# Contextual attention: straight-line loops, exponentials written twice, and a shifted addition done by an accumulating DMA

## The reference

```python
raw_w, Hr, Wr = _extract_patches(b, kernel, RATE * STRIDE)   # 4x4 patches, step 2
f = b[:, :, ::RATE, ::RATE]                                  # 40x40
w, Hs, Ws = _extract_patches(f, KSIZE, STRIDE)               # 3x3 patches of f
norm = jnp.sqrt(jnp.sum(w * w, axis=(2, 3, 4), keepdims=True))
wn = (w / jnp.maximum(norm, ESCAPE)).reshape(B, L, C * KSIZE * KSIZE)
yi = jnp.einsum('bpd,bld->blp', xf, wn) * mm
yi = jax.nn.softmax(yi * SOFTMAX_SCALE, axis=1) * mm
patches = jnp.einsum('blp,bld->bpd', yi, raw_w.reshape(B, L, C * kernel * kernel))
# overlapping 4x4 patches are added up at step 2, and the sum is divided by 4
```

## Time and profile before

| | us |
|---|---|
| median of 3 runs | 1543.32 (1543.14 to 1550.75) |
| the profiled execution | 1549.3 |
| its span, first to last instruction | 1547.5 |
| TensorE busy | 1389.9 |
| VectorE busy | 1226.9 |
| ScalarE busy | 860.8 |
| GpSimd busy | 54.6 |

### The profile page before, as it was taken

How to read it: one execution, slowest core, us unless ns; L and a number is a source line. 1 busy time by engine, 2 the same in 40 slices (tenths; PEclk the granted TensorE clock), 3 DMA queues, 4 the chain that set the end, 5 groups by cost and what they waited for, 6 DMA issues and landing times.

```text
span 1547.5 us, 28187 instructions
## 1 busy us (share of the span) xinstructions
PE 1389.9 (90%) x7190; PEld 906.0 (59%) x7190; DVE 1226.9 (79%) x2831; ACT 860.8 (56%) x2233; POOL 54.6 (4%) x63
## 2 busy tenths in 40 slices
PE   4978999889998899988999889997999889999896
PEld 4755655656557565565656566565665656556333
DVE  4668888778888788887898777977779788887983
ACT  2676555646557465583555644656545655557431
POOL 1001000010000100001000000001000010000100
PEclk9998999999999999999999999998999999999998
DMA  5305352273522653145631545315462153522442
GB/s 97 44 1 152 96 119 73 61 161 86 114 66 78 153 105 104 50 108 134 122 87 45 130 113 116 86 51 138 106 120 76 50 148 92 120 66 81 124 137 60
DMA packets 181676, 149.67 MB, mean 97 GB/s; under 512 B 119986, under 2 KB 177394, under 8 KB 181490
## 3 DMA queue, kind: packets, MB, share of 16 engines
q1 hardware_dynamic: 181170, 146.60, 39.8%
q10 hardware_dynamic: 320, 0.99, 0.3%
HBM read 19.76 MB, written 13.11 MB: 21 GB/s over the span
## 4 chain that ended last, share of the span: by engine, by line
PE 40%; DVE 18%; issue 13%; SPq 12%; ACT 8%; DMA 6%; DVEq 1%; ACTq 1%; POOL 0%; POOLq 0%
PE psO L511 18%; PE psG L461 17%; SPq L307 5%; DVE G L921 4%; DVE G L861 4%; DVE S L867 3%; DMA SH<-G 3%; PE psG L470 3%; DVE Z L954 3%; ACT S L680 3%; DVE G L932 3%; SPq L255 3%; SPq L295 2%; DMA HV<-LOHI 2%; ACT G L666 2%
## 5 line engine op out<-in xcount | busy, mean ns | idle before, releaser
L511 PE MATMUL psO<-Z,B 123*128 123x492 f32 (+1 forms) x1792 | 768.0, 557 | 41.8 <-ACT OSB L700 22.6
L511 PEld LDWEIGHTS psO<-Z,B 123*128 123x128 f32 x1792 | 327.5, 195 | 266.7 <-issue 179.5
L461 PE MATMUL psG<-LH,HL 128*123 128x246 f16 (+2 forms) x2616 | 411.0, 287 | 26.2 <-issue 19.7
L461 PEld LDWEIGHTS psG<-LH,HL 128*123 128x123 f16 x2616 | 280.5, 138 | 166.2 <-issue 112.5
L867 DVE CUSTOM_DVE_ANT_0 S<-G,RB 123x492 f32<-123x492 f32 (+1 forms) x448 | 268.9, 606 | 94.4 <-DVE G L861 53.9
L691 ACT ACTIVATE G<-G,nb 123x492 f32<-123x492 f32 (+1 forms) x448 | 270.2, 649 | 106.7 <-DVE G L921 105.9
L680 ACT ACTIVATE S<-S,nm 123x480 f32<-123x480 f32 (+3 forms) x560 | 306.7, 553 | 4.2 <-DVE nm L872 4.1
L921 DVE SCALAR_TENSOR_TENSOR G<-G,RA,psB 123x492 f32<-123x492 f32 (+1 forms) x448 | 275.2, 657 | 20.5 <-issue 19.6
L932 DVE TENSOR_TENSOR G<-G,SH 123x492 f32<-123x492 f32 (+1 forms) x448 | 251.4, 600 | 42.9 <-DMA SH<-G 42.5
L666 ACT ACTIVATE G<-psG 123x492 f32<-123x492 f32 (+3 forms) x256 | 120.3, 473 | 216.1 <-PE psG L461 127.4
L653 ACT ACTIVATE G<-psG 123x246 f32<-123x246 f32 (+1 forms) x136 | 64.4, 474 | 262.5 <-PE psG L461 262.2
(11 more groups left out here) (84 smaller groups left out, 585.7 us busy)
## 6 DMA issues: line engine op xcount, KB each, us to landing
SH<-G SPq DMA_DIRECT2D x336, 214.8 KB
SH<-G SPq DMA_DIRECT2D x112, 107.2 KB
SH<-G SPq DMA_DIRECT2D x336, 19.2 KB
XP<-x SPq DMA_DIRECT2D x20, 280.0 KB, 6.0
XP<-mid SPq DMA_DIRECT2D x20, 280.0 KB, 5.3
mid<-OSB SPq DMA_DIRECT2D x52, 80.0 KB, 2.3
out<-OSB SPq DMA_DIRECT2D x52, 80.0 KB, 2.3
HL<-LOHI SPq DMA_DIRECT2D x16, 246.5 KB, 3.5
```

Of the source, the lines that this page charges most:

```text
L461: last = pe.matmul(psG[0:TW, bank, b0 * TW:b1 * TW], st[:, p:p + TW], mv[:, lo:lo + n], start=i == 0, stop=i == len(terms) - 1)
L511: last = pe.matmul(psO[:, b, 0:n], B[:, o:o + 128], Z[:, 2 * (s % 2) + j, 0:n], start=t == 0, stop=t == TILES - 1)
```

## The change

There are two parts. All loops over units are written out: `Fori` becomes `for` on all engines. And the shifted addition is done in another way. ScalarE now makes each exponential twice: first into a buffer `Y` (four of them, where `SH` was), then in place in `G`. GpSimd issues a DMA that *adds* `Y`, moved by one partition and one column, to `G` (`accum_op=ALU.add`), one DMA of 122 rows per tile. `shift_pair` on SyncE and `add_shifted` on VectorE are gone. Who waited for `y1_made` (VectorE's count) now waits for the landing of the DMAs, `y1_in`, by the tile's buffer. ScalarE waits, before it writes a `Y` buffer, for the landing of the DMA four tiles earlier.

```diff
             def softmax_pair(at):   # ScalarE
                 for j, t in enumerate(arg_tiles(i)):
-                    act.wait_ge(arg_made, u * NB + k * TILES + 2 * i + j + 1)
-                    act.sem_inc(act_gate, 1)
+                    o = k * TILES + 2 * i + j
+                    if u * NB + o >= SFREE:
+
+                        act.wait_ge(*y1_done(u, o - SFREE))
+                        act.sem_inc(act_gate, 1)
+                    act.wait_ge(arg_made, u * NB + o + 1)
+                    act.activation(Y[:, o % SFREE, 0:n], G[:, t * GLEN + c0:t * GLEN + c0 + n], ACT.Exp,
+                                   bias=nb[:, bass.ds(u * TILES + t, 1)]).then_inc(y_copied, 1)
+                for j, t in enumerate(arg_tiles(i)):
+                    act.wait_ge(y_copied, u * NB + k * TILES + 2 * i + j + 1)
                     y = G[:, t * GLEN + c0:t * GLEN + c0 + n]
                     act.activation(y, y, ACT.Exp, bias=nb[:, bass.ds(u * TILES + t, 1)]).then_inc(y_made, 1)
...
-            with act.Fori(0, UNITS - 2) as u:
+            for u in range(UNITS - 2):
                 body(u, u + 1, u + 2)
...
-            def add_shifted(at):   # VectorE
-                for j, t in enumerate(arg_tiles(i)):
-                    o = k * TILES + 2 * i + j
-                    dve.wait_ge(sh_in[o % SFREE], (u * (NB // SFREE) + o // SFREE + 1) * 16 * len(SHIFT_PARTS))
-                    g = G[:, t * GLEN + c0:t * GLEN + c0 + n]
-                    dve.tensor_tensor(g, g, SH[:, o % SFREE, 0:n], ALU.add).then_inc(y1_made, 1)
...
             def sum_pair(at, s):
-                dve.wait_ge(y1_made, u * NB + k * TILES + min(2 * i + 3, TILES) + SFREE)
-                dve.sem_inc(dve_gate, 1)
+
+                for o in range(2 * i + 1, min(2 * i + 3, TILES)):
+                    dve.wait_ge(*y1_done(u, k * TILES + o))
+                    dve.sem_inc(dve_gate, 1)
...
-                pool.wait_ge(y1_made, u * NB + 2 * i + 2 + SFREE)   # GpSimd, wrap
-                pool.sem_inc(pool_gate, 1)
+                for o in (2 * i, 2 * i + 1):
+                    pool.wait_ge(*y1_done(u, o))
+                    pool.sem_inc(pool_gate, 1)
...
+            def add_shifted(at):   # GpSimd
+                u, k, i = at
+                c0, n = p_cols(k)
+                for j, t in enumerate(arg_tiles(i)):
+                    o = k * TILES + 2 * i + j
+                    g = t * GLEN + c0
+                    pool.wait_ge(y_made, u * NB + o + 1)
+                    pool.dma_start(G[1:TW, g + 1:g + n], Y[0:TW - 1, o % SFREE, 0:n - 1],
+                                   accum_op=ALU.add).then_inc(y1_in[o % SFREE], 16)
+
             def body(u, v):
                 for s in BODY:
+                    at = place(u, v, s + LEAD)
+                    if at:
+                        add_shifted(at)
                     if s < 5 and u is not None:
                         wrap(u, s + 2)
```

More of the change, by code:

```diff
@@ L106, in contextual_attention @@
         RB = sb("RB", [TW, TILES * TW], F32)
-        SH = sb("SH", [TW, SFREE, 4 * TW], F32)
+        Y = sb("Y", [TW, SFREE, 4 * TW], F32)
         SHJ = sb("SHJ", [TW, 4 * TW], F32)
@@ L190, in contextual_attention @@
         arg_made = sem("arg_made")
+        y_copied = sem("y_copied")
         y_made = sem("y_made")
-        sh_in = [sem(f"sh_in{i}") for i in range(SFREE)]
+        y1_in = [sem(f"y1_in{i}") for i in range(SFREE)]
         shj_in = sem("shj_in")
-        y1_made = sem("y1_made")
         z_made = sem("z_made")
@@ L202, in contextual_attention @@
         SQ_STEPS = 4
-        CLEARED = 10
+        CLEARED = 9
         MROWS = HALF + 1
@@ L219, in arg_tiles, with y1_done @@
             return [(2 * i + TILES - 1) % TILES, 2 * i]
+        def y1_done(u, o):
+            return y1_in[o % SFREE], (u * (NB // SFREE) + o // SFREE + 1) * 16
         def place(u, v, s):
@@ L312, in shift_strip @@
                 c0, n = p_cols(k, True)
-                sp.wait_ge(y1_made, u * NB + k * TILES + 1 + SFREE)
+                sp.wait_ge(*y1_done(u, k * TILES))
                 sp.sem_inc(sp_gate, 1)
@@ L329, in body @@
                         lay_out_features(w, ("HL", "LH", "H1", "HV"))
-                    at = place(u, v, s + LEAD)
-                    if at:
-                        shift_pair(at)
                     at = place(u, v, s + 2)
@@ L341, in body, with source @@
                             store_chunk(u, NK - 1, dst)
[L343 to L346, removed]
+            def source(u):
+                return None if u is None else (x, mid)[u // IMAGES][u % IMAGES]
             sp.sem_inc(stored, 16)
@@ L360, in _ @@
             xp_read(0)
[L361 to L369, removed]
+            body(None, 0, 1, source(1), source(0), None)
+            for u in range(UNITS):
+                v, w = (n if n < UNITS else None for n in (u + 1, u + 2))
+                body(u, v, w, source(w), source(v), (mid, out)[u // IMAGES][u % IMAGES])
             sp.wait_ge(stored, (UNITS * sum(N_OUT) + 1) * 16)
@@ L573, in _ @@
             body(None, 0, 1)
-            with pe.Fori(0, UNITS - 2) as u:
+            for u in range(UNITS - 2):
                 body(u, u + 1, u + 2)
@@ L963, in body @@
                         argument_pair(at)
-                    at_y = place(u, v, s + AHEAD)
-                    if at_y:
-                        add_shifted(at_y)
                     at_z = place(u, v, s + 1)
@@ L1037, in _ @@
             body(None, 0, 1)
-            with dve.Fori(0, UNITS - 2) as u:
+            for u in range(UNITS - 2):
                 body(u, u + 1, u + 2)
@@ L1070, in _ @@
             body(None, 0)
-            with pool.Fori(0, UNITS - 1) as u:
+            for u in range(UNITS - 1):
                 body(u, u + 1)
```

17 lines of the change are left out of this document (1 added, 16 removed).

## The result

The changed kernel takes 1602.4 us in the median (1596.0 to 1606.1) where the kernel before takes 1543.9 on the same chip: 1.0364 times as long [1.0315, 1.0414]. The forecast was 1517, faster, so its direction was wrong. The profiled execution has a span of 1604.3 us against 1547.5, 56.8 more.

The account below looks back on a forecast made before the run. TensorE was taken as the limit for most of each unit, ScalarE in short pieces, TensorE's jump between looped units. 1549.3 - 19.5 (loops) + 3 (units) - 10 (last unit) = 1522.8, less 6.0 for the median: 1517 us, range 1497 to 1700.

Parts of the forecast that it names:

- Ends: 17 us, if the layout DMAs land about half a microsecond later beside heavier transfers: Handover between units: low end of the gain from written-out loops; 19.5 us was taken, 22 the other end.
- 12.6 us of engine time for 234 KB: DMA engine time of one addition at 18.5 GB/s per engine: 0.8 us over sixteen engines, 6.3 over two.
- are not queued behind those issues, though they share the engines: Once per unit, new DMAs avoid the wait on SyncE behind the next image's rows: -1 us, seven times -7.
- I take 2.1 to 3 us: Last unit: flight of an adding DMA, within a round of about 6 to 7 us for two pairs.
- +3 us: Inside the units: chunk 3 pieces +10, squares pair +2.4, two score pairs -2.6, shifted copies -7; ends -10 and +20.
- The squares pair: Pair with the next image's squares: ScalarE adds 1.3 us where 0.9 is free, +0.4, six times +2.4.
- The pair with two score pairs: Mid-unit pair: VectorE falls to 5.2 us, ScalarE rises to 6.7 and takes its place; -0.4, seven times -2.6.
- I take 19.5: Handover between units: gain in us from removing TensorE's five jumps back, with ends of 17 and 22.
- -7: Once per unit, shifted copies stand on SyncE behind the next image's rows, costing TensorE about 1 us; seven times -1.
- the second: Rival, chance 0.14: GpSimd's issue is dear, setting the last unit's pace from 1.66 us; 1569 us at 2.68.
- the third: Rival, chance 0.11: jumps return as fetch stalls, or ScalarE's cost mid-unit equals the loops' gain; 1536 to 1544 us.
- The first (two engines per addition): Rival, chance 0.20: each addition's DMA gets two engines, lengthening flight to 7.6 or 13.9 us; mostly 1566 to 1850 us.

Follow-up runs that it names:

- With copies: The changed kernel with plain copies of the same bytes in place of all adding DMAs (addition left out): 1527.8 us, 0.9880 of the kernel before.
- the loops alone: The kernel before with `Fori` written out as a Python `for` on all five engines, nothing else changed: 1505.5 us, 0.9746 of the kernel before.
- exponentials of one column: The changed kernel with ScalarE's exponential into Y covering one column in place of up to 492, adding DMAs whole: 1584.9 us, 1.0262 of the kernel before.

## Why the prediction was wrong

**The failing step: "Ends: 17 us, if the layout DMAs land about half a microsecond later beside heavier transfers".** The layout was named as what is late next, but its delay was bounded by half a microsecond. It was about 9 us per handover, 64 in all, and alone it turns the sign: with plain copies in the four pairs beside the layout the kernel takes 0.9962 of the time before. The evidence stood in the rows: the handover's DMA share was 0.70 over 15.66 us, and the DMA share was read only in a mid-unit stretch with 0.27, where there is room. The forecast's own 12.6 us of engine time for 234 KB, doubled for an addition as the runs showed it, would have given 8 x 25.2 / 16 = 12.6 us for the four pairs beside the layout; 11.1 were measured. The copies of before kept out of the layout only by their order on SyncE; the forecast counted the freed SyncE as a gain and did not ask what its order had held apart. It said of the new DMAs, where it spoke of the row loads, that they "are not queued behind those issues, though they share the engines", and priced only the first half of that sentence.

**The flight in the last unit, "I take 2.1 to 3 us".** It is 6.5 us. The exponentials and the issue were shorter on that path than taken (1.3 and 0.6 us for 2.6 and 1.27), and still the round became 8.95 in place of 6 to 7, and the last unit gained 1.5 us in place of 10. With copies it takes 99.3 us, close to the 95 to 98 that were worked out: the mechanism was right, the size of the flight was not.

**ScalarE, "+3 us" within the units.** From the loops alone to the copies the units lose 0.6 + 0.3 + 0.7 + 0.4 + 2.8 = 4.8 us each, 33 in all. The squares pair came as forecast (+0.4). In the last chunk three pairs pay, 2.8 us, where two were counted with 1.4. The third, 1.3 us, lies where the next unit's first output product waits for ScalarE's `read_out`, with two more exponentials ahead of it. With the loops alone, then after:

```profile
493.51 0.78 ACT L697 ACTIVATE OSB<-psO 128x328 f32<-128x328 f32 x2
...
494.39 1.48 PE L508 MATMUL psO<-Z,B 123*128 123x492 f32 x3 [1.94 <-issue]
```
```profile
528.88 0.80 ACT L690 ACTIVATE OSB<-psO 128x328 f32<-128x328 f32 x2
...
529.78 2.22 PE L493 MATMUL psO<-Z,B 123*128 123x492 f32 x3 [3.26 <-issue]
```

The profile names no releaser; the products start 0.1 us after the second `read_out` ends in both. Another 3.6 us, before the first output of all, have no term in the sum; with exponentials of one column they are gone (131.6 us). The pair with two score pairs rose by 0.6 us where it was to fall by 0.4.

**The loops, "I take 19.5".** TensorE's part was about right (24 us by itself, 20 to 31 by its interval); the other engines' loops, 18 us more, were missed, though VectorE's stops stood in the earlier trace rows, as 19.6 us of "issue" before L921. This error helped: had the loops given only the 19.5, the result would have been slower still.

**The sum.** In spans the forecast had -19.5 + 3 - 10 = -26.5 us. The columns of the table give -43.0 for the loops in the seven units, +33.4 there for the doubled exponentials, +64.3 for the late layout, -1.5 for the last unit and +3.5 before the first output, together +56.7.

**Shifted copies behind the row loads, "-7".** Pair 11 did fall, from 8.04 to 7.57 us, but as much with the loops alone, where the copies still stand behind those issues.

**Which rival.** None of the three. GpSimd's issue takes 0.98 us, so the second falls. No stop came back in the longer code, and ScalarE's 33 us do not eat the loops' 43, so the third falls too. The first (two engines per addition) gave "slower" by another way. That 1602 us lies in its range, and in the wide range of 1497 to 1700 us that was made from it, is luck. In the trace an addition's 26.0 us of engine time landed 5.7 us after its issue in the median:

```profile
G<-Y POOLq DMA_DIRECT2D x336, 234.0 KB, 5.7
```

With one packet at a time on an engine that takes at least 26.0 / 5.7 = 4.6 engines; and 0.4 us after the first packet of a pair, before the issue of the second addition has ended, 16 packets are in flight at once (median). The Trainium skill, "DMA: Bandwidth & Descriptors", section "Why a DMA increments its semaphore by 16 and not by 1", has a rule by which 122 rows get two engines; this trace does not agree with it, and fits the exception better that the section names for some direct copies issued by GpSimd. The Trainium skill, "Collectives: The Full Stack", section "The bandwidth ceiling: the fold count and why AG ≠ RS ≠ AR", says of the adding step of a collective that it reads two sources on one ring and so runs at half the rate of the copying one; the DMAs of this kernel agree, 26.0 against 12.5 us. The forecast weighed it for the flight alone (3 us on the sum) and not for the engines it would share.

## What to carry to other kernels

Before adding load to the DMA engines, look at the DMA share of the stretch in which a transfer is waited for, not of the span: at 0.9, in these runs, every microsecond of sixteen engines' time that was added there was about a microsecond of delay. Add what a wait costs behind it: TensorE came back from its wait at half its clock. A queue in program order can be what keeps two transfers apart; work that is moved to another engine's queue loses that order. An adding DMA took the engine time of two copies (26.0 against 12.5 us), and the engine work that it saves counts only where that engine is the limit.

## What the runs showed of the hardware

The issue of an addition by GpSimd takes 984 ns and that of a copy of the same bytes 531; the copies leave as 26,880 packets and the additions as 64,512. SyncE's own issue of the same layout DMA stretches from 0.60 to 2.95 us while the engines are full (share 0.97). And a jump back stops VectorE and ScalarE about as long as TensorE: TensorE's branch itself is recorded with 3.9 us, VectorE's and ScalarE's with 0.07 and 0.05, but VectorE's next instruction comes 3.2 to 4.1 us after the one before the branch and ScalarE's queue goes on after 3.7 to 4.3. GpSimd's goes on after 0.1 us.
